# Moving half of the low part's products behind the next slot's minus points in a fused convolution kernel

## The reference, cut to what matters

```python
x = x + silu(bn(sum_e routing[b, e] * conv3x3(_gn(x), w_experts[e])))   # routing = sigmoid(mean(gn(x)) @ w_route.T + b_route)
x = x + conv3x3(_gn(x), sign(W))
```

## Time and profile before

| | us |
|---|---|
| median of 3 runs | 277.41 |
| the profiled execution | 278.55 |
| its span, first to last instruction | 276.8 |

### The profile page before, as it was taken

The page is one execution under the profiler, slowest core; times in us unless marked ns, Lnnn a source line. Parts: engine busy times, 40 slices in busy tenths (PEclk is TensorE's granted clock), DMA queues, the critical chain, the costliest instruction groups (busy, mean ns, idle before and its releaser), DMA issues.

```text
span 276.8 us, 4049 instructions
## 1 busy us (share of the span) xinstructions
PE 269.0 (97%) x1322; PEld 187.2 (68%) x1322; DVE 253.9 (92%) x466; ACT 208.0 (75%) x419; POOL 50.6 (18%) x61
## 2 busy tenths in 40 slices
PE   8999989999999999999999999999999999999993
PEld 7854846858586776848576675948567684957663
DVE  5879999999999999999999999999998999996885
ACT  2487988888869788796978898696988885725770
POOL 2000011212122041414112021413203121210110
PEclk9999999999999999999999999999999999999999
DMA  6999925453625544361645545262555535263407
GB/s 228 390 376 313 294 119 152 55 99 89 127 90 76 152 77 111 62 133 78 100 128 78 152 76 117 55 116 96 80 150 77 145 57 105 86 118 102 76 0 154
DMA packets 11253, 35.20 MB, mean 127 GB/s; under 512 B 1248, under 2 KB 3424, under 8 KB 11232
## 3 DMA queue, kind: packets, MB, share of 16 engines
q0 software_dynamic: 4176, 15.21, 32.6%
q1 hardware_dynamic: 6768, 19.47, 18.9%
q10 hardware_dynamic: 288, 0.26, 0.3%
HBM read 11.34 MB, written 16.25 MB: 100 GB/s over the span
## 4 chain that ended last, share of the span: by engine, by line
PE 79%; DVE 8%; ACT 6%; DMA 3%; issue 2%; POOL 1%; SPq 0%; DVEq 0%; ACTq 0%
PE pc L525 36%; PE pa L490 12%; PE pb L490 12%; PE pe_ L490 11%; PE pd L480 4%; DMA X<-y 2%; DMA X<-x 1%; PE pd L434 1%; DVE U L1054 1%; PE ps L460 1%; ACT xn L776 1%; POOL rstd L394 1%; ACT y L828 1%; DVE U L1044 1%; PE ps L464 1%
## 5 line engine op out<-in xcount | busy, mean ns | idle before, releaser
L1054 DVE SCALAR_TENSOR_TENSOR U<-we,route,U 128x1152 f32<-128x1152 f32 x45 | 63.7, 1415 | 0.1
L525 PE MATMUL pc<-lo,ws 128*128 128x496 f16 (+3 forms) x270 | 61.6, 374 | 0.0
L525 PE MATMUL pc<-hi,ws 128*128 128x496 f16 (+3 forms) x270 | 59.8, 375 | 0.2 <-ACT hi L837 0.2
L394 POOL TENSOR_TENSOR rstd<-ve,nhalf 128x2 f32<-128x2 f32 (+1 forms) x19 | 23.4, 1231 | 139.4 <-ACT ve L753 137.9
L525 PEld LDWEIGHTS pc<-hi,ws 128*128 128x128 f16 x270 | 26.4, 98 | 29.7 <-issue 0.6
L525 PEld LDWEIGHTS pc<-lo,ws 128*128 128x128 f16 x270 | 26.6, 106 | 24.6
L490 PE MATMUL pa<-V,UM 128*128 128x256 f32 (+1 forms) x180 | 41.8, 382 | 0.0
L490 PE MATMUL pe_<-V,U 128*128 128x256 f32 (+1 forms) x180 | 40.6, 375 | 0.0
L490 PE MATMUL pb<-V,UM 128*128 128x256 f32 (+1 forms) x180 | 40.5, 375 | 0.0
L490 PEld LDWEIGHTS pb<-V,UM 128*128 128x128 f32 x180 | 34.2, 190 | 5.4 <-issue 0.5
L490 PEld LDWEIGHTS pe_<-V,U 128*128 128x128 f32 x180 | 34.1, 190 | 3.8
(11 more groups left out here) (152 smaller groups left out, 414.4 us busy)
## 6 DMA issues: line engine op xcount, KB each, us to landing
X<-x SPq DMA_DIRECT2D x15, 512.0 KB, 5.1
out<-X SPq DMA_DIRECT2D x15, 512.0 KB, 2.6
out<-ev POOLq DMA_DIRECT2D x15, 512.0 KB, 5.5
X<-y POOLq DMA_DIRECT2D x14, 512.0 KB, 4.5
we<-w_experts SPq DMA_DIRECT2D x3, 768.0 KB, 8.3
ws_raw<-w_sign SPq DMA_DIRECT2D x1, 576.0 KB, 11.4
out<-X SPq DMA_DIRECT2D x1, 384.0 KB, 2.4
X<-x ACTq DMA_DIRECT2D x2, 128.0 KB, 3.0
```

The lines of the kernel that those rows point to most:

```text
L394: g.tensor_tensor(rstd[:, c, a:b], ve[:, c, a:b], nhalf[:, a:b], ALU.pow).then_inc(rstd_ready, 1)
L525: mm = mm_(rows[:, r0 - first // W:r1 - first // W, c0:c1], ws[:, tap * C:(tap + 1) * C], plane((hi, lo)[part], i)[:, r0 + ky - 1:r1 + ky ...
L1054: v.scalar_tensor_tensor(out=flat(U[i % RING][:]), in0=flat(we[:, e, :, :]), scalar=route[:, i, e:e + 1], in1=flat(U[i % RING][:]), op0=AL ...
```

## The change

From slot 3 on, the lower half of the low part of image t-1 is not multiplied at the end of slot t, but in slot t+1 behind `minus_points`, with `group_vars` between its eighth and its ninth tap. `group_means(c+1)` goes between the sixth and the seventh tap of the upper half. On ACT `mean_in` goes ahead of `silu`, and `var_in` ahead of the routing. On DVE the second mix goes ahead of the inverse transform from slot 3 on, and `pool_routes` ahead of `low_part` in all slots.

```diff
@@ tensor
                     minus_points(t)
                     if t == 1:
                         group_means(c)
+                    elif t == 2:
+                        group_vars(c)
                     else:
+
+                        sign_half(t - 2, 1, 1, TAP_ORDER[:8])
                         group_vars(c)
+                        sign_half(t - 2, 1, 1, TAP_ORDER[8:])
                     plus_points(t)
@@
-                    sign_half(t - 1, 1, 0)
-                    group_means(c + 1)
-                    sign_half(t - 1, 1, 1)
+                    if t == 1:
+                        sign_half(t - 1, 1, 0)
+                        group_means(c + 1)
+                        sign_half(t - 1, 1, 1)
+                    else:
+                        sign_half(t - 1, 1, 0, TAP_ORDER[:6])
+                        group_means(c + 1)
+                        sign_half(t - 1, 1, 0, TAP_ORDER[6:])
@@ scalar
                 if c < B:
                     normalise(c)
+                if t > 2 and c + 1 < B:
+                    mean_in(c + 1)
                 silu(t)
                 if t < B - 1:
                     mean_mid(t)
-                if c + 1 < B:
+                if t <= 2:
                     mean_in(c + 1)
+                elif c + 1 < B:
+                    var_in(c + 1)
                 if c < B:
                     routing(c)
                     mix(c)
-                if c + 1 < B:
+                if t <= 2:
                     var_in(c + 1)
@@ vector
                 mix(t + 1, 1)
+                if t > 2:
+                    mix(t + 1, 2)
                 inverse_sums(t)
                 inverse_inner(t)
                 inverse_outer(t)
+                pool_routes(t + LAG - 1)
                 low_part(t - 1)
-                mix(t + 1, 2)
-                pool_routes(t + LAG - 1)
+                if t <= 2:
+                    mix(t + 1, 2)
                 mix(t + 1, 3)
```

## The result

| | median us | range | runs |
|---|---|---|---|
| before | 277.73 | 276.71 to 278.58 | 19 |
| changed | 278.75 | 277.99 to 280.97 | 19 |

The ratio is 1.0036 with a 95% interval of 1.0022 to 1.0049: about 1.0 us slower, where 1.3 us faster was forecast.

A forecast was written before the change was run, and what follows sets the result against it. PE was taken to set the pace, slots starting 15.73 us apart. The terms -0.11 (start), -0.96 (slots) and -0.3 (late landing) sum to -1.37; 277.41 - 1.37 = 276.0, stated as 276.1, range 275.0 to 278.8.

The forecast's parts named there:

- is paid by the vars product's later place and the faster rstd: ACT/POOL/DMA loop: the 1.04 us of mean_in ahead of silu is offset, leaving room 0.35 against about 0.15 before.
- A: Rival: POOL's rstd is held through both DVE mixes, spread is 0.85 late; slower, 280.2 us; chance 15%.
- B: Rival: small waits, 0.1 in each of ten slots, or vars costing 0.2, eat the gain; 277.0 to 277.4; chance 22%.
- Slots of 15.65, -0.96 for slots 4 to 15: PE: group_vars between fp16 taps saves 0.08 us a slot, -0.96 over 12 slots.
- S: The start of a slot's pb on PE, from which the forecast counts times within the slot.
- Room 0.35 in the settled slots: Group_vars' weight load: loop through ACT, POOL and DMA is ready at S + 19.35, PE wants it at S + 19.70.
- Start, -0.11: First slots: PE gains 1.4 us by earlier pooled, but waits for var_mid and kernel rows leave 0.11 at slot 3's pa.
- In slot 4, where DVE is still 0.4 late, the room is about 0.0: ACT/POOL/DMA loop in slot 4: no room left before PE waits for spread; no cost in the sum.
- Late landing of slot 12, -0.3: DMA X<-y landing 0.6 late in slot 12 costs PE 0.2 to 0.3 rather than 0.5; -0.3, bounds 0 and -0.37.

The follow-up runs named there:

- e7: e1 with group_vars placed behind the ninth tap instead of between the eighth and ninth; 278.06 us, ratio 1.0012 to the kernel before.
- e1: The changed kernel with ScalarE's (ACT's) order as before, PE and DVE as changed; 277.18 us, ratio 0.9981 to the kernel before.
- e5: e1 with PE's lower half moved only from slot 4 on; 276.56 us, ratio 0.9949 to the kernel before.
- e10: e5 again, the same kernel on another chip; 276.77 us, ratio 0.9978 to the kernel before.
- e3: The kernel before with only ScalarE's (ACT's) order changed, PE and DVE as before; 277.96 us, ratio 0.9999 to the kernel before.

## Why the prediction was wrong

By the trace the forecast of -1.37 became +0.74. The step that failed is that moving `mean_in` ahead of `silu` "is paid by the vars product's later place and the faster rstd", with a room of 0.35 in the settled slots and of "about 0.0" in slot 4 behind which no cost was put. The settled room was 0.17, and slots 4, 5 and 7 cost 1.5 us. That 278.75 still lies within the stated 275.0 to 278.8 is luck: the upper end was drawn for rivals A and B. The terms, each as put and as found:

- **Slots of 15.65, -0.96 for slots 4 to 15: right.** 15.64, `pa` 2.54, -0.087 a slot or -1.04 in all, and e7 shows that it is the cause named. The settled loop is right up to the DMA: in slot 9 of the changed kernel (pb at 154.93) rstd started at 159.67 for 1.25, S + 4.74 to S + 5.99 (forecast 4.8 and 5.98), and `X<-y` was issued at 167.65, S + 12.72, as the sum gave (11.1 + 1.62).
- **Room 0.35 in the settled slots: wrong by half.** The weight load begins 0.37 ahead of the product's place in the chain (174.44 against 174.81), not 0.2, so PE wants it at S + 19.51, not at S + 19.70:

```profile
173.74 0.48 ACT L744 ACTIVATE spread<-dev,var 128x1 f32<-128x1 f32 x2
...
174.44 0.39 PEld L460 LDWEIGHTS ps<-spread,gmat 128*128 128x128 f32 x2
```

`spread` ended 0.22 ahead of the load, and where the load waits it follows by 0.05: the room is 0.17, hardly more than the 0.15 of the kernel before. In e1 it is 0.71 in the same slot (`spread` ended at 173.33, the load began at 174.09). So `mean_in` ahead of `silu` took 0.54 of it.

- **Start, -0.11: wrong by 0.39.** Slot 2 already leaves out its lower half, and slot 3 is the first to do the half of the slot before. `pa` of slot 3 ends 0.28 later than before (66.70 - 40.40 against 67.55 - 41.53), not 0.11 earlier. Two costs were left out. `pool_routes` had stood between the second and third mix in slots 1 and 2; without it the two dependent mixes follow each other (2.86 for two, as in the earlier trace rows), 0.1 more in each slot on the one engine that is busy without a gap up to there. And a `pb` that starts after a wait takes 2.77, not 2.54. The wait for the kernel rows was foreseen; that PE could have filled it with the half taken away was not, and e5 shows it.
- **"In slot 4, where DVE is still 0.4 late, the room is about 0.0": put at nothing in the sum.** The sum went on as if every slot were the settled one. `pb` of slot 3 ended 0.4 later than forecast; POOL came not in the middle of a first mix but 0.1 behind its start and was held for all of it, 1.87 against the 1.15 that I took from the earlier trace rows; the landing was 5.13 against 4.53. That is 0.7 and 0.6 on a room that had been put at nothing: 0.97 in slot 4, 0.42 in slot 5, and in slot 7 another 0.12 (rstd 1.61 in slot 6), 1.51 in all. e1, with an rstd as long, takes it away by taking 1.04 out of the same loop.
- **Late landing of slot 12, -0.3: wrong.** PE lost 0.38 there as before; a landing 0.6 late doesn't fit into a room of 0.17. Only with `mean_in` out of the loop is it covered: e1, e5 and e10 have no late weight load there, though e10's DMA took 5.17.

The sum closes: -0.11 + 0.39 - 1.04 + 1.51 = 0.75, against 0.74 measured.

Of the rivals, A (rstd held through both mixes) did not happen: no rstd of the changed kernel took more than 1.91, and from slot 3 on POOL always got in between the two mixes, each rstd ending 0.57 behind the first. (A's price was 0.2 short besides: two mixes from S + 4.0 end at S + 6.87, and by the earlier trace rows a held rstd ends 0.57 later, at S + 7.4, not 7.2.) POOL doesn't get in between in every case: in slot 2 of the changed kernel it came at 47.97 under one of DVE's row transforms, was held through that one and the next two, and ended at 49.62. The port lock of the Trainium skill (SBUF — State Buffer, "SBUF: two separate sides") agrees with the rstd held by the mix in flight, 1.87 in slot 3; for the 2.01 of the earlier trace rows and the 1.65 of slot 2, where an operation that started after POOL's went first, it doesn't say who is next. B, small waits that eat the gain, was the right rival with too small a price, a few events instead of an even drizzle, and its bad end had been given too little chance.

Still open: by the times the changed kernel is 1.0 us slower and e5 0.6 (e10) to 1.4 faster than before, by the stretch 0.8 slower and 1.6 faster. All variants but e3 look better in the trace than in the times, by 0.1 to 1.0; e3 looks 0.5 worse. With one profile of the kernel before, I can't say how much of that is this one execution.

## What to carry to other kernels

When an engine at 97% is tied into a loop through four others, the loop's room in the settled slots isn't the room that decides: work it out for the first slots after a new order begins, where the engines are out of phase, and give each "about zero" a price. An instruction that merely fills a neighbour's wait belongs behind the loop's own work even if it fits most of the time. And where work is moved from one slot into the next, don't begin in a slot that is followed by a wait which that work would have filled.

## What the runs showed of the hardware

**The accumulating DMA lands late only where an instruction packet lies in its time.** Over the fourteen profiles there are 196 `X<-y` transfers of 512 KB. In 146 no packet of an instruction queue lay between issue and `var_mid`, and they took 4.51 to 4.70 us. In 36 there was a packet of queue q8, and they took 4.57 to 5.22; all 12 that took more than 5.0 us are among them. With one of queue q14 (14 cases) it was 4.55 to 4.81. From the DMA view of the late transfer of slot 3 in the changed kernel, and of the same transfer before:

```profile
q0 software_dynamic: 144, 0.52, 54.5%
q8 instruction: 1, 0.02, 1.1%
```

```profile
q0 software_dynamic: 144, 0.52, 60.5%
```

Transfers with a single instruction packet of 0.02 MB thus took up to 0.6 us longer, though not all did (4.57 in slot 3 of e3). Which transfers have one was the same in all three executions of the changed kernel and in both of e5's, and the kernel before had none in slot 3. This is a correlation; no run moved the packet alone. It would explain why a change that only reorders work can make one DMA late in each execution.

**A tie of hundredths decides 1.3 us.** In the kernel before, POOL's rstd takes 0.71 in slot 9, where it starts at 160.02 and the mix at 160.04, and 2.01 in slot 5, where the starts are as far apart, 97.11 and 97.13. Across the variants it takes values all the way between (0.83 where POOL came 1.16 behind the mix's start, 1.87 at 0.12), according to how much of the mix is left when POOL comes.

**The head of the kernel varies by up to 3 us** between executions (first `X<-y` at 40.4 to 41.6 in thirteen profiles and 43.6 in e7's), more than the change moved. A difference of one profile's spans says nothing here.
